# The output projection of a linear-attention stage in three bf16 passes, with its low half made first in GpSimd's step

## The chip, the cores and the metric

The kernel runs on one core of a Trainium2 chip. The metric is the device time of one execution in microseconds (us). A core has five engines with queues of their own: TensorE (PE; its weight loads are shown as PEld), VectorE (DVE), ScalarE (ACT), GpSimd (POOL) and SyncE (SP). Each works through its instructions strictly in order, and engines wait for one another by semaphores.

## The reference, cut to what matters

`x` is 128 sequences of 64 tokens with 256 channels, all f32. Two layers follow: L0 (attention and a feed-forward part, both with adaptive layer norm) and L1, a linear attention with a gated, modulated output:

```
xn = layer_norm(x, norm_g, norm_b)
q, k, v = xn @ Wq + bq, xn @ Wk + bk, xn @ Wv + bv      # 16 heads of 16 channels
q = softmax over the channels of a head;  k = softmax over the tokens
ctx = k^T v (per sequence and head);      y = q ctx
scale, shift = split(silu(emb) @ emb_W + emb_b)
h = layer_norm(y, sn_g, sn_b) * (1 + scale) + shift
h = silu(h) @ out_W + out_b                             # the projection that the change is about
x = x + gate_msa * h
```

## The kernel before, in words

Tokens lie on the 128 partitions, two sequences to a tile, so there are 64 tiles of 128 tokens by 256 channels. All of `x` stays on the core (`x_all`). Four stages follow each other: setup, an attention pass (to about 540 us), a feed-forward pass (to about 890 us), and the linear pass, `linear_pass`, for L1. A matmul whose operands are split into bf16 high and low halves runs as three passes, `SPLITS` = high by high, high by low, low by high.

In a pass, the order of work is a table written by hand for each engine. `pipeline(eng, [(lag, stage), ...])` walks over steps; in step s each listed stage, in the order of the list, is given tile s - lag. Since an engine keeps its order, the list is also the order in which its work queues up. Steps at both ends are written out, and those between run in a loop of four steps a turn.

In the linear pass, one step of each engine before the change is this (the number is the lag):

- TensorE: `k_v_first` 6 (L1545), `turn_kq` 5 (L1565, the transposes of the softmaxed k and q), `turn_x` 0 (L1594), `k_v_second` 6 (L1545), `project` 11 (L1515 and L1517), `qkv` 2 (L1573, L1576, then k in L1582, L1585), `q_kv` 7 (L1536), `turn_y` 8 (L1525).
- GpSimd: `softmax` 5 (L1403, L1405), `inverse_deviations` -1 (L1427, L1430), `silus` 10 (L1395, then L1397), `add` 12 (L1387).
- ScalarE: `x3_high` 1 (L1503), `v_high` 3 (L1497), `load_gate` 9 (issues two DMAs, L1443), `k_high` 5 (L1470), `q_copy` 5 (L1475), `k_exponentials` 3 (L1489), `modulate` 9 (L1458), `q_exponentials` 3 (L1479), `store` 13 (L1449), `tanhs` 9 (L1465).
- VectorE: `statistics`, `x3_low` 1 (L1709), `k_maxima`, `y_statistics`, `q_maxima`, `aggregate`, `q_lower`, `v_low`, `y_aggregate` 8 (L1620), `mask` 6 (L1633), `k_low`, `hat` -1 (L1702), `total` 4, `y_hats` 8, `residual` 11 (L1607).

How the stages hang together: `turn_kq` waits for `softmax` of the same step. `k_high` waits for `turn_kq`. `x3_high` writes a buffer with two slots, and so waits until `qkv` of the step before has done with k (`k_done`). `x3_low` waits for `x3_high`. `inverse_deviations` waits for `y_aggregate` (the second of the two values that it turns is y's), `hat` for `inverse_deviations`, and `mask` for `k_v_second` of its step. `silus` computes (tanh + 1) * z; its result, f32, is the stationary operand of `project` against the f32 weights `w_out3`. The projection's weights are loaded by SyncE at the start of the feed-forward pass, straight into their place. In that pass, stage `split_qvk3` (in its step for block 2) splits the weights of q, v and k in two, the high half on ScalarE and the low half on VectorE.

Of the kernel before, what the change touches and what calls it, by code (L numbers as in the profile page):

```python
# [23 lines left out]
ALU = mybir.AluOpType  # L24
ACT = mybir.ActivationFunctionType
# [86 lines left out]
class Shared:  # L112


    def __init__(self, nc, ctx):
        def sb(name, shape, dt):
            return ctx.enter_context(nc.sbuf_tensor(name, shape, dt))
# [18 lines left out]
        self.w_out3 = sb("w_out3", [P, NC_, C], F32)  # L136
# [782 lines left out]
def feed_forward_pass(nc, m, wq, wk, wv, bq, bk, bv, out_w):  # L919
# [5 lines left out]
    with ExitStack() as ctx:  # L925
# [8 lines left out]
        biases3_high, biases3_mid = m.w_qkv[:, HI, 0, :], m.w_qkv[:, HI, 1, :]  # L934
        b_norm3_wide = m.fc_full[:, 6 * C:6 * C + NC_ * P].rearrange("p (c n) -> p c n", c=NC_)
# [16 lines left out]
        qvk3_here = sem("qvk3_here")  # L952
        qvk3_hi_made = sem("qvk3_hi_made")
# [38 lines left out]
        @block.sync  # L992
        def _(sp):
            sp.dma_start(m.w_out3[:], out_w.rearrange(CHUNKED, p=P)).then_inc(m.linear_here, 16)
            for k, source in enumerate((wq, wv, wk)):
                sp.dma_start(qvk3_full[:, :, k * C:(k + 1) * C], source.rearrange(CHUNKED, p=P)).then_inc(qvk3_here, 16)
            for k, source in enumerate((bq, bv, bk)):
                sp.dma_start(biases3[:, k * C:(k + 1) * C], source[None, :].to_broadcast([P, C])).then_inc(qvk3_here, 16)
            sp.wait_ge(m.linear_here, 16)
# [44 lines left out]
        def _(act):  # L1044
# [9 lines left out]
            def split_qvk3(t):  # L1054

                if isinstance(t.n, int) and t.n == 2:
                    act.wait_ge(qvk3_here, 16 * 6)
                    act.wait_ge(norm3_widened, 2)
                    for c in range(NC_):
                        act.activation(m.w_qvk3[:, HI, c, 0:2 * C], qvk3_full[:, c, 0:2 * C], ACT.Identity,  # L1060
                                       scale=m.g_norm3[:, c:c + 1]).then_inc(qvk3_hi_made, 1)
                        act.activation(m.w_qvk3[:, HI, c, 2 * C:3 * C], qvk3_full[:, c, 2 * C:3 * C], ACT.Identity,
                                       scale=minus_g_norm3[:, c:c + 1]).then_inc(qvk3_hi_made, 1)
# [86 lines left out]
        def _(dve):  # L1150
# [82 lines left out]
            def split_qvk3(t):  # L1233

                if isinstance(t.n, int) and t.n == 2:
                    dve.wait_ge(qvk3_hi_made, 2 * NC_)
# [32 lines left out]
def linear_pass(nc, m, cond, out):  # L1269
# [5 lines left out]
    with ExitStack() as ctx:  # L1275
# [30 lines left out]
        silu = sb("silu", [P, NC_, P])  # L1306
        gate = sb("gate", [P, C], F32, 4)
# [46 lines left out]
        silu_made = sem("silu_made")  # L1354
        out_done = sem("out_done")
# [27 lines left out]
        def _(pool):  # L1383
# [6 lines left out]
            def silus(t):  # L1390
# [3 lines left out]
                reuse(pool, out_done, t, 2)  # L1394
                pool.tensor_tensor(silu[a][:], tanh[a][:], z_t[a][:], ALU.mult).then_inc(silu_product, 1)  # L1395
                pool.wait_ge(silu_product, t.n + 1)
                pool.tensor_tensor(silu[a][:], silu[a][:], z_t[a][:], ALU.add).then_inc(silu_made, 1)  # L1397

# [26 lines left out]
            def power(a, which, nth):  # L1425
# [7 lines left out]
            pipeline(pool, [(5, softmax), (-1, inverse_deviations), (Y_LAG, last_inverse_deviations),  # L1433
                            (10, silus), (12, add)])

        @block.scalar
        def _(act):
# [38 lines left out]

            def q_exponentials(t):
# [21 lines left out]
            def x3_high(t):  # L1499
# [5 lines left out]
            pipeline(act, [(1, x3_high), (3, v_high), (9, load_gate), (5, k_high), (5, q_copy),  # L1505
                           (3, k_exponentials), (9, modulate), (3, q_exponentials), (13, store),
# [3 lines left out]
        def _(pe):  # L1510
            def project(t):
                a = t.slot(2)
                pe.wait_ge(silu_made, t.n + 1)
                reuse(pe, branch_made, t, 1)
                pe.matmul(ps_out[:], m.ones[:], m.rows_out3, start=True, stop=False)  # L1515
                for c in range(NC_):
                    last = pe.matmul(ps_out[:], silu[a][:, c], m.w_out3[:, c], start=False, stop=(c == NC_ - 1))  # L1517
# [79 lines left out]
            pipeline(pe, [(6, k_v_first), (5, turn_kq), (0, turn_x), (6, k_v_second), (11, project), (2, qkv), (7, q_kv),  # L1597
# [3 lines left out]
        def _(dve):  # L1601
# [103 lines left out]
            def x3_low(t):  # L1705
# [8 lines left out]
                           (11, residual)])  # L1714
# [45 lines left out]
```

## Time and profile before

| | |
|---|---|
| median of 3 runs | 1313.19 us (1313.13 to 1314.98) |
| the profiled execution's own time | 1312.1 us |
| its span, first to last instruction | 1310.4 us |
| busy: PE, PEld | 1172.7 us (89%), 858.6 us (66%) |
| busy: DVE, ACT, POOL | 943.8 us (72%), 783.9 us (60%), 844.5 us (64%) |
| mean granted TensorE clock | 0.975 of full speed |

The busy figures are means over stages that differ much. Matmuls are pipelined and their ends are modelled, so what a matmul costs in a stream is read from the starts of neighbouring groups rather than from its own duration. On the other engines a record's duration can overlap the next start by some hundredths of a microsecond, so there too spacings between starts are the better measure. An idle time in brackets stands ahead of the instruction that ended it, with the one that released it.

### The profile page before, as it was taken

What the parts mean: (1) busy time and instruction counts of PE and PEld (TensorE: products, weight loads), DVE (VectorE), ACT (ScalarE), POOL (GpSimd) and SP (SyncE); (2) the same over time, 40 slices, a digit from 0 to 9 for tenths busy, and PEclk for the clock granted to TensorE, in tenths of its full rate; (3) what the DMA queues carried; (4) which work ended last, traced back from release to release, by engine and by line L of the source; (5) the groups of instructions that cost most, each with busy time, mean ns of one, the idle gap of its engine ahead of it and who ended that gap; (6) DMA issues with size and microseconds to landing.
All of it is one profiled execution on the core that took longest, in us unless ns stands there. A gap on an engine that the chain in (4) does not pass through costs nothing. (4 is left out here: it accounts for less than half of the span.)

```text
span 1310.4 us, 37657 instructions
## 1 busy us (share of the span) xinstructions
PE 1172.7 (89%) x12222; PEld 858.6 (66%) x12222; DVE 943.8 (72%) x2272; ACT 783.9 (60%) x2143; POOL 844.5 (64%) x1017
## 2 busy tenths in 40 slices
PE   3687889899899874999999999986999999999996
PEld 2466777777777763566666666663666666666664
DVE  6666788788788754646464656435899999999984
ACT  2666677677677762635454544523676676776764
POOL 4577677777777764546666667532466676676667
PEclk8899999999999997899999999997999999999999
DMA  7562323323323332000101010100011111111112
GB/s 243 142 147 50 60 57 55 61 55 56 65 51 59 60 56 72 17 28 22 33 16 32 16 32 16 33 17 1 17 39 37 40 52 37 39 52 39 45 48 73
DMA packets 138511, 67.85 MB, mean 52 GB/s; under 512 B 76368, under 2 KB 137168, under 8 KB 138448
## 3 DMA queue, kind: packets, MB, share of 16 engines
q1 hardware_dynamic: 109904, 40.92, 14.6%
q10 hardware_dynamic: 28544, 26.12, 6.6%
q8 instruction: 35, 0.57, 0.2%
q14 instruction: 28, 0.23, 0.1%
HBM read 41.31 MB, written 8.65 MB: 38 GB/s over the span
## 5 line engine op out<-in xcount | busy, mean ns | idle before, releaser
L1123 PE MATMUL f_ps_h<-f_x_split,w_fc 128*128 128x512 bf16 x768 | 173.2, 383 | 2.2 <-DVE f_biases L1249 1.2
L1096 PE MATMUL f_ps_y<-w_fc,f_h_split 128*128 128x256 bf16 x1536 | 172.7, 273 | 2.3 <-DVE f_branch L1215 2.3
L1096 PEld LDWEIGHTS f_ps_y<-w_fc,f_h_split 128*128 128x128 bf16 x1536 | 150.2, 98 | 23.6 <-issue 3.0
L634 POOL TENSOR_TENSOR e_split<-e_full,e_split 128x1024 bf16<-128x1024 f32 x64 | 136.5, 2134 | 33.5 <-ACT e_full L707 32.3
L1223 DVE TENSOR_TENSOR f_h_split<-f_h,f_h_split 128x512 bf16<-128x512 f32 x64 | 64.1, 1004 | 103.9 <-ACT f_h L1082 103.9
L1123 PEld LDWEIGHTS f_ps_h<-f_x_split,w_fc 128*128 128x128 bf16 x768 | 75.5, 99 | 88.9 <-issue 3.0
L1081 ACT ACTIVATE f_h_split<-f_ps_h,columns 128x512 bf16<-128x512 f32 x128 | 89.0, 695 | 66.3 <-POOL f_h_split L1038 36.3
L767 PE MATMUL ps_s<-qk_t,k_pairs 128*128 128x64 bf16 x3072 | 102.4, 195 | 12.7 <-DMA k_pairs<-qk_t 10.6
L767 PEld LDWEIGHTS ps_s<-qk_t,k_pairs 128*128 128x128 bf16 x3072 | 99.8, 99 | 15.5 <-DMA k_pairs<-qk_t 12.2
L614 POOL TENSOR_TENSOR x_split<-x_t,x_split 128x256 bf16<-128x256 f32 x64 | 44.5, 695 | 95.3 <-ACT x_split L655 95.3
L1427 POOL TENSOR_TENSOR l_rstd<-l_mean_var,eps_norm 128x2 f32<-128x2 f32 (+1 forms) x73 | 14.1, 193 | 140.2 <-DVE l_mean_var L1620 108.9
L1038 POOL TENSOR_TENSOR f_h_split<-f_h,f_h_split 128x512 bf16<-128x512 f32 x64 | 79.7, 1256 | 36.5 <-ACT f_h L1082 36.5
L786 PE MATMUL ps_qk<-w_qkv,x_split 128*128 128x512 bf16 x384 | 95.5, 386 | 0.4 <-POOL x_split L614 0.4
L1576 PE MATMUL l_ps_qv<-w_qvk,l_x_split 128*128 128x512 bf16 x384 | 95.8, 387 | 0.0
L1082 ACT ACTIVATE f_h<-f_ps_h,columns 128x512 f32<-128x512 f32 x128 | 89.5, 699 | 0.0
L1069 ACT ACTIVATE f_x_split<-f_x 128x1024 bf16<-128x1024 f32 x16 | 16.9, 1058 | 118.6 <-POOL f_x L1005 114.5
L1458 ACT ACTIVATE l_z_t<-l_ps_yt,shift,scale 128x64 f32<-128x64 f32 x256 | 84.4, 441 | 4.7 <-PE l_ps_yt L1525 3.7
L667 ACT ACTIVATE v_split<-ps_v 128x256 bf16<-128x256 f32 x64 | 24.7, 386 | 101.5 <-DMA v_pairs<-v_split 80.9
L702 ACT ACTIVATE e_split<-ps_s,minus_shift 128x1024 bf16<-128x1024 f32 x64 | 71.4, 1115 | 12.8 <-PE ps_s L767 12.5
L1489 ACT ACTIVATE l_kq<-l_ps_k,l_k_tops 128x64 f32<-128x64 f32 x256 | 77.0, 327 | 0.6 <-DVE l_k_tops L1655 0.5
L1470 ACT ACTIVATE l_k_t<-l_ps_kq 128x256 bf16<-128x256 f32 x64 | 24.5, 383 | 88.0 <-PE l_ps_kq L1565 87.9
L707 ACT ACTIVATE e_full<-ps_s,minus_shift 128x1024 f32<-128x1024 f32 x64 | 70.9, 1107 | 0.0
(182 smaller groups left out, 3285.3 us busy)
## 6 DMA issues: line engine op xcount, KB each, us to landing
v_pairs<-v_split SPq DMA_DIRECT2D x128, 66.0 KB, 2.1
k_pairs<-qk_t SPq DMA_DIRECT2D x256, 32.0 KB, 2.3
gain<-gammas SPq DMA_DIRECT2D x64, 128.0 KB, 3.0
f_gain<-gammas ACTq DMA_DIRECT2D x32, 256.0 KB, 4.2
l_gate<-in_cond ACTq DMA_DIRECT2D x128, 64.0 KB, 2.5
out<-x_all ACTq DMA_DIRECT2D x16, 512.0 KB, 3.0
x_all<-in_x SPq DMA_DIRECT2D x13, 512.0 KB, 5.4
fc_full<-in_L_cond_fc_w SPq DMA_DIRECT2D x2, 1024.0 KB, 7.6
```

Source lines behind the costliest of these rows:

```text
L634: pool.tensor_tensor(flat(e_split[a][:, LO]), flat(e_full[:]), flat(e_split[a][:, HI]), ALU.subtract).then_inc(e_lo_made, 1)
L702: act.activation(flat(e_split[a][:, HI]), flat(ps_s[:]), ACT.Exp, bias=m.minus_shift[:])
L767: last = pe.matmul(ps_s[:, s, G_ * c + g], k_pairs[:, t.slot(4), k, c, s, g].rearrange("p r k -> p (r k)"), qk_t[:, 0, t.slot(4), q, c, s ...
L786: last = pe.matmul(ps_qk[:, :], x1_split[a][:, xs, c, :], m.w_qkv[:, ws, c, 0:2 * C], start=(i == 0 and c == 0), stop=(i == 2 and c == NC_ ...
L1038: pool.tensor_tensor(h_split[a][:, LO, f], h[f % 4][:], h_split[a][:, HI, f], ALU.subtract).then_inc(h_lo_odd, 1)
L1081: act.activation(h_split[a][:, HI, f], ps_h[f % 4][:], ACT.Gelu, bias=m.b_fc1[:, f:f + 1])
L1082: act.activation(h[f % 4][:], ps_h[f % 4][:], ACT.Gelu, bias=m.b_fc1[:, f:f + 1]).then_inc(h_made, 1)
L1096: last = pe.matmul(ps_y[:, i], h_split[a][:, hs, f, i * P:(i + 1) * P], m.w_fc2[:, ws, f], start=(f == 0 and k == 0), stop=(f == F_CHUNKS ...
L1123: last = pe.matmul(ps_h[f % 4][:], m.w_fc1[:, ws, c, f * P:(f + 1) * P], x2_split[a][:, xs, c], start=(k == 0 and c == 0), stop=(k == 2 an ...
L1458: act.activation(z_t[a][:, c, s * L:(s + 1) * L], ps_yt[:, c, s * L:(s + 1) * L], ACT.Identity, bias=by_seq(m.shift3, c, t, s), scale=by_s ...
L1489: act.activation(kq[t.slot(4)][:, i * L:(i + 1) * L], ps_k[:, c, s * L:(s + 1) * L], ACT.Exp, bias=k_tops[a][:, c, s:s + 1], scale=-1.0, a ...
L1576: last = pe.matmul(ps_qv[:], x3_split[a][:, xs, c], m.w_qvk3[:, ws, c, 0:2 * C], start=False, stop=(i == 2 and c == NC_ - 1))
```

## The change

The f32 weights `w_out3` become a pair of bf16 halves. The f32 array is now loaded into `out3_full` in the feed-forward pass and split there, high half on ScalarE, low half on VectorE, ahead of the pieces of `split_qvk3`. In the linear pass the silu is split too: `silu_high` on ScalarE at lag 10, between `q_exponentials` and `tanhs`; `silu_low` on GpSimd at lag 11, as the first stage of its step. `project` then runs three bf16 passes over two chunks, six matmuls, in place of two f32 ones, and moves from lag 11 to 12; `residual` 11 to 12, `add` 12 to 13, `store` 13 to 14, `load_gate` 9 to 10.

```diff
-        self.w_out3 = sb("w_out3", [P, NC_, C], F32)
+        self.w_out3 = sb("w_out3", [P, 2, NC_, C], BF16)
...
-            sp.dma_start(m.w_out3[:], out_w.rearrange(CHUNKED, p=P)).then_inc(m.linear_here, 16)
+            sp.dma_start(out3_full[:], out_w.rearrange(CHUNKED, p=P)).then_inc(out3_here, 16)
...
-            sp.wait_ge(m.linear_here, 16)
+            sp.wait_ge(qvk3_here, 16 * 6)
...
                 if isinstance(t.n, int) and t.n == 2:
+                    act.wait_ge(out3_here, 16)
+                    act.activation(m.w_out3[:, HI], out3_full[:], ACT.Copy).then_inc(out3_hi_made, 1)
...
                 if isinstance(t.n, int) and t.n == 2:
+                    dve.wait_ge(out3_hi_made, 1)
+                    dve.tensor_tensor(m.w_out3[:, LO], out3_full[:], m.w_out3[:, HI], ALU.subtract)
...
                 pool.wait_ge(tanh_made, t.n + 1)
-                reuse(pool, out_done, t, 2)
+                reuse(pool, silu_lo_made, t, 2)
...
+            def silu_low(t):
+                a = t.slot(2)
+                pool.wait_ge(silu_hi_made, t.n + 1)
+                reuse(pool, out_done, t, 2)
+                pool.tensor_tensor(silu_split[a][:, LO], silu[a][:], silu_split[a][:, HI], ALU.subtract
+                                   ).then_inc(silu_lo_made, 1)
...
-            pipeline(pool, [(5, softmax), (-1, inverse_deviations), (Y_LAG, last_inverse_deviations),
-                            (10, silus), (12, add)])
+            pipeline(pool, [(11, silu_low), (5, softmax), (-1, inverse_deviations), (Y_LAG, last_inverse_deviations),
+                            (10, silus), (13, add)])
...
+            def silu_high(t):
+                a = t.slot(2)
+                act.wait_ge(silu_made, t.n + 1)
+                reuse(act, out_done, t, 2)
+                act.activation(silu_split[a][:, HI], silu[a][:], ACT.Copy).then_inc(silu_hi_made, 1)
...
-            pipeline(act, [(1, x3_high), (3, v_high), (9, load_gate), (5, k_high), (5, q_copy),
-                           (3, k_exponentials), (9, modulate), (3, q_exponentials), (13, store),
+            pipeline(act, [(1, x3_high), (3, v_high), (10, load_gate), (5, k_high), (5, q_copy),
+                           (3, k_exponentials), (9, modulate), (3, q_exponentials), (10, silu_high), (14, store),
                            (9, tanhs)])
...
-                pe.wait_ge(silu_made, t.n + 1)
+                pe.wait_ge(silu_lo_made, t.n + 1)
                 reuse(pe, branch_made, t, 1)
                 pe.matmul(ps_out[:], m.ones[:], m.rows_out3, start=True, stop=False)
-                for c in range(NC_):
-                    last = pe.matmul(ps_out[:], silu[a][:, c], m.w_out3[:, c], start=False, stop=(c == NC_ - 1))
+                for i, (zs, ws) in enumerate(SPLITS):
+                    for c in range(NC_):
+                        last = pe.matmul(ps_out[:], silu_split[a][:, zs, c], m.w_out3[:, ws, c],
+                                         start=False, stop=(i == 2 and c == NC_ - 1))
...
-            pipeline(pe, [(6, k_v_first), (5, turn_kq), (0, turn_x), (6, k_v_second), (11, project), (2, qkv), (7, q_kv),
+            pipeline(pe, [(6, k_v_first), (5, turn_kq), (0, turn_x), (6, k_v_second), (12, project), (2, qkv), (7, q_kv),
```

How this moves the instructions: first GpSimd, in the steps written out just ahead of the loop. Before, a step there (`silus`, `add`, then the next step's `softmax` and the two instructions for the inverse deviations) reads

```order
L1395 TENSOR_TENSOR l_silu<-l_tanh,l_z_t 128x256
L1397 TENSOR_TENSOR l_silu<-l_silu,l_z_t 128x256
L1387 TENSOR_TENSOR x_all<-x_all,l_branch 128x256
L1403 TENSOR_TENSOR l_kq<-l_kq,l_sums 128x256
L1405 TENSOR_TENSOR l_kq<-l_kq,l_sums 128x256
L1427 TENSOR_TENSOR l_rstd<-l_mean_var,eps_norm 128x2
```

and with the change (line numbers are the changed kernel's)

```order
L1405 TENSOR_TENSOR l_silu<-l_tanh,l_z_t 128x256
L1407 TENSOR_TENSOR l_silu<-l_silu,l_z_t 128x256
L1397 TENSOR_TENSOR x_all<-x_all,l_branch 128x256
L1413 TENSOR_TENSOR l_silu_split<-l_silu,l_silu_split 128x256
L1420 TENSOR_TENSOR l_kq<-l_kq,l_sums 128x256
L1422 TENSOR_TENSOR l_kq<-l_kq,l_sums 128x256
L1444 TENSOR_TENSOR l_rstd<-l_mean_var,eps_norm 128x2
```

One subtraction, L1413, now stands between the last instruction of a step (the sum into `x_all`) and the softmax of the next.

Second, ScalarE in the same place, the end of a step and the start of the next. Before:

```order
L1470 ACTIVATE l_k_t<-l_ps_kq 128x256
L1475 ACTIVATE l_q_t<-l_ps_kq 128x256
L1489 ACTIVATE l_kq,l_sums<-l_ps_k,l_k_tops 128x64 x4
L1458 ACTIVATE l_z_t<-l_ps_yt,shift,scale 128x64 x4
L1479 ACTIVATE l_kq<-l_kq 128x256
L1465 ACTIVATE l_tanh<-l_z_t 128x256
L1503 ACTIVATE l_x_split<-l_ps_xt 128x256
```

and with the change

```order
L1487 ACTIVATE l_k_t<-l_ps_kq 128x256
L1492 ACTIVATE l_q_t<-l_ps_kq 128x256
L1512 ACTIVATE l_kq,l_sums<-l_ps_k,l_k_tops 128x64 x4
L1475 ACTIVATE l_z_t<-l_ps_yt,shift,scale 128x64 x4
L1502 ACTIVATE l_kq<-l_kq 128x256
L1498 ACTIVATE l_silu_split<-l_silu 128x256
L1482 ACTIVATE l_tanh<-l_z_t 128x256
L1526 ACTIVATE l_x_split<-l_ps_xt 128x256
```

The copy that makes the high half, L1498, stands behind `q_exponentials` and ahead of the tanh. On TensorE nothing changes its place within a step: the pair L1515, L1517 x2 becomes L1538, L1541 x6.

## Rows read from the trace of the kernel before

**Rows 1.** Busy time by stretch: start:end us, span, then each engine, clock, DMA.

```profile
core 0: us, PE busy (x) PEld busy (x) DVE busy (x) ACT busy (x) POOL busy (x), PEclk, DMA share, GB/s
...
540.00:800.00 260.00, 257.90 (x1782) 175.93 (x1781) 147.38 (x236) 127.91 (x208) 162.40 (x107) 1.00 0.09 25
...
1000.00:1050.00 50.00, 49.67 (x441) 34.09 (x439) 47.23 (x131) 35.55 (x149) 34.42 (x59) 1.00 0.16 48
```

**Rows 2.** Timeline of one steady step: start us, us, engine, line, op [idle before].

```profile
1009.58 0.66 PE L1565 MATMUL l_ps_kq<-ident,l_kq 128*128 128x128 f32 x4
...
1010.27 0.38 ACT L1470 ACTIVATE l_k_t<-l_ps_kq 128x256 bf16<-128x256 f32 x1 [1.37 <-PE l_ps_kq L1565]
...
1010.82 0.28 PE L1515 MATMUL l_ps_out<-bias_rows,ones 128*128 128x256 bf16 x1
...
1010.93 0.69 DVE L1633 TENSOR_TENSOR l_kv<-l_ps_kv,same_head 128x512 f32<-128x512 f32 x1
...
1011.03 0.19 POOL L1427 TENSOR_TENSOR l_rstd<-l_mean_var,eps_norm 128x2 f32<-128x2 f32 x1 [1.60 <-DVE l_mean_var L1620]
...
1011.81 0.38 PE L1573 MATMUL l_ps_qv<-bias_rows,ones 128*128 128x512 bf16 x1
...
1011.97 0.73 POOL L1395 TENSOR_TENSOR l_silu<-l_tanh,l_z_t 128x256 f32<-128x256 f32 x1
...
1012.04 0.81 DVE L1702 TENSOR_SCALAR l_x_hat<-x_all,l_mean_var,l_rstd 128x256 f32 x1
...
1012.77 0.73 POOL L1397 TENSOR_TENSOR l_silu<-l_silu,l_z_t 128x256 f32<-128x256 f32 x1
...
1013.43 0.47 ACT L1465 ACTIVATE l_tanh<-l_z_t 128x256 f32<-128x256 f32 x1
...
1014.15 0.61 POOL L1403 TENSOR_TENSOR l_kq<-l_kq,l_sums 128x256 f32<-128x256 f32 x1
...
1014.36 0.38 ACT L1503 ACTIVATE l_x_split<-l_ps_xt 128x256 bf16<-128x256 f32 x1 [0.46 <-PE l_ps_k L1585]
...
1014.72 0.62 POOL L1405 TENSOR_TENSOR l_kq<-l_kq,l_sums 128x256 f32<-128x256 f32 x1
1014.78 0.42 DVE L1709 TENSOR_TENSOR l_x_split<-l_ps_xt,l_x_split 128x256 bf16<-128x256 f32 x1 [0.18 <-ACT l_x_split L1503]
...
1015.59 0.66 PE L1565 MATMUL l_ps_kq<-ident,l_kq 128*128 128x128 f32 x4
...
1017.24 0.19 POOL L1427 TENSOR_TENSOR l_rstd<-l_mean_var,eps_norm 128x2 f32<-128x2 f32 x1 [1.90 <-DVE l_mean_var L1620]
```

**Rows 3.** Timeline of the feed-forward pass: a stream of bf16 matmuls of 256 columns.

```profile
822.33 5.40 PE L1096 MATMUL f_ps_y<-w_fc,f_h_split 128*128 128x256 bf16 x48
```

**Rows 4.** Costliest groups, form by form: like operations; xcount, busy us, mean ns, idle before.

```profile
L655 ACT ACTIVATE x_split<-x_t 128x256 bf16<-128x256 f32 x64 | 26.2, 410 | 0.1
...
L1060 ACT ACTIVATE w_qvk<-fc_full,columns 128x512 bf16<-128x512 f32 x2 | 1.5, 750 | 0.0
...
L1223 DVE TENSOR_TENSOR f_h_split<-f_h,f_h_split 128x512 bf16<-128x512 f32 x64 | 64.1, 1004 | 103.9 <-ACT f_h L1082 103.9
...
L614 POOL TENSOR_TENSOR x_split<-x_t,x_split 128x256 bf16<-128x256 f32 x64 | 44.5, 695 | 95.3 <-ACT x_split L655 95.3
```

**Rows 5.** Timeline, ScalarE: the k copy of steps 11 and 66, 55 steps apart.

```profile
943.34 0.38 ACT L1470 ACTIVATE l_k_t<-l_ps_kq 128x256 bf16<-128x256 f32 x1 [1.96 <-PE l_ps_kq L1565]
...
1277.51 0.38 ACT L1470 ACTIVATE l_k_t<-l_ps_kq 128x256 bf16<-128x256 f32 x1 [1.90 <-PE l_ps_kq L1565]
```

**Rows 6.** Timeline, the last steps of the pass.

```profile
1301.66 0.72 POOL L1397 TENSOR_TENSOR l_silu<-l_silu,l_z_t 128x256 f32<-128x256 f32 x1
...
1303.83 0.72 POOL L1397 TENSOR_TENSOR l_silu<-l_silu,l_z_t 128x256 f32<-128x256 f32 x1
...
1304.60 0.28 PE L1515 MATMUL l_ps_out<-bias_rows,ones 128*128 128x256 bf16 x1 [1.02 <-POOL l_silu L1397]
...
1305.79 0.42 DVE L1607 TENSOR_TENSOR l_branch<-l_ps_out,l_gate 128x256 f32<-128x256 f32 x1 [1.74 <-PE l_ps_out L1517]
```

**Rows 7.** Timeline of an early step of the pass, where GpSimd is idle beside it.

```profile
928.23 0.41 DVE L1702 TENSOR_SCALAR l_x_hat<-x_all,l_mean_var,l_rstd 128x256 f32<-128x256 f32 x1 [0.27 <-POOL l_rstd L1430]
```

More of the change, by code:

```diff
@@ L934, in feed_forward_pass @@
         biases3_high, biases3_mid = m.w_qkv[:, HI, 0, :], m.w_qkv[:, HI, 1, :]
+        out3_full = sb("out3_full", [P, NC_, C], F32, 1)[0]
         b_norm3_wide = m.fc_full[:, 6 * C:6 * C + NC_ * P].rearrange("p (c n) -> p c n", c=NC_)
@@ L952, in feed_forward_pass @@
         qvk3_here = sem("qvk3_here")
+        out3_here = sem("out3_here")
+        out3_hi_made = sem("out3_hi_made")
         qvk3_hi_made = sem("qvk3_hi_made")
@@ L1306, in linear_pass @@
         silu = sb("silu", [P, NC_, P])
+        silu_split = sb("silu_split", [P, 2, NC_, P], BF16)
         gate = sb("gate", [P, C], F32, 4)
@@ L1354, in linear_pass @@
         silu_made = sem("silu_made")
+        silu_hi_made = sem("silu_hi_made")
+        silu_lo_made = sem("silu_lo_made")
         out_done = sem("out_done")
@@ L1713, in _ @@
                            (6, mask), (5, k_low), (-1, hat), (4, total), (Y_LAG, y_hats),
-                           (11, residual)])
+                           (12, residual)])
 _INS = ["x", "cond_1024", "L0_cond_mat_qkv_w", "L0_cond_q_bias", "L0_cond_v_bias", "L0_cond_scale_mul",
```

## The prediction

> **What bounds the kernel now.** I read the busy times by stretch first, since the page's means mix four stages. In the linear pass TensorE is busy 49.67 of 50 us and VectorE 47.23; ScalarE (35.55) and GpSimd (34.42) look as if they had room [rows 1]. The reader should not stop there: where GpSimd has its room decides this case. The timeline of one step, read next, shows it [rows 2]. GpSimd works without a break from L1427 (start 1011.03) through the silu, the sum and the two softmax products, whose last ends at 1014.72 + 0.62 = 1015.34. Then it idles 1.90 us, until VectorE has y's mean, and starts the next L1427 at 1017.24. All its slack lies *behind* the softmax. TensorE's transposes L1565, which wait for that softmax, start at 1015.59, a quarter of a microsecond after it. So an instruction put ahead of the softmax has 0.25 us of cover, and one put behind it would have 1.9 us.
>
> From one L1565 to the next it is 1015.59 - 1009.58 = 6.01 us; over the 55 steps from 11 to 66 the mean is (1277.51 - 943.34) / 55 = 6.08 [rows 2, 5]. I follow one further ring, because it passes through all engines and takes two steps: L1565 to `x3_high` (which ScalarE starts when TensorE has done with k: 0.46 us idle ahead of it) is 1014.36 - 1009.58 = 4.78; to `x3_low` 0.42; to the next L1427 1017.24 - 1014.78 = 2.46; L1427 to the softmax 1014.15 - 1011.03 = 3.12; the softmax itself 1.19 (1014.15 to 1015.34); GpSimd to TensorE 0.05 (in the last steps L1515 starts at 1304.60, and L1397, from 1303.83 for 0.72, ends at 1304.55 [rows 6]). The sum is 12.02, two steps, or 6.01 a step [rows 2]. So this ring stands level with TensorE's own stream: whatever is added to it shows, halved, in every step.
>
> **The change, part by part.**
>
> *TensorE's gain.* The projection takes 1011.81 - 1010.82 = 0.99 us of the stream, bias row included [rows 2]. A bf16 matmul of the same 256 columns costs 5.40 / 48 = 0.11 us in a stream [rows 3]; seven (bias and six) are 0.77. Gain 0.22 us a step, which shortens TensorE's stream to 5.79 and the 4.78 of the ring to 4.56.
>
> *GpSimd's subtraction.* The same form, 128x256 f32 into bf16, takes 0.695 us [rows 4]; records overlap the next by some 0.04 (1014.72 - 1014.15 = 0.57 for a product of 0.61), so 0.66. It stands ahead of the softmax, past the 0.25 us of cover. Of the ring above it makes 12.02 - 0.22 + 0.66 = 12.46, or **6.23 us a step**.
>
> *The new wait.* `silu_low` also waits for `silu_high`, and behind it in GpSimd's queue stand the softmax, and behind that L1565. This closes a ring of one step that was not there: L1565 to `k_high` 1010.27 - 1009.58 = 0.69; `k_high` to the place of `silu_high`, where L1465 starts now, 1013.43 - 1010.27 = 3.16; `silu_high` itself 0.41 (an f32 SBUF tile of that size into bf16 on ScalarE [rows 4]); to GpSimd about 0.08; the subtraction 0.66; the softmax 1.19; to TensorE 0.05. Sum **6.24 us a step** [rows 2, 4]. The 0.08 is an estimate between the 0.05 above and the 0.1 or so that L1427 lags behind VectorE. Bounds of this ring: 6.15 with 0.38 for `silu_high` (as L1503 takes from PSUM) and the subtraction hidden to 0.61, 6.32 with 0.47 (as L1465 takes).
>
> `silu_high`'s own input is in time: the silu is complete 1012.77 + 0.73 - 1011.03 = 2.47 us after L1427, and ScalarE comes to it 3.85 us after L1565, which is some 1.2 to 1.4 us ahead of L1427. ScalarE gives `silu_high` some 0.3 us, taken from the 0.46 that it idles ahead of `x3_high`; with k done 0.22 us earlier the two nearly meet, and I cost it at nothing. Were that cover gone, `x3_low` would be late and VectorE with it.
>
> *Both rings* give 6.23 and 6.24. The steady pass ran 0.07 above its ring before (6.08 against 6.01, loop turns and waits that alternate). TensorE and ScalarE now have slack over a loop turn, so I add only part of that, 0.05: 6.29. Over 55 steps: 55 x (6.29 - 6.08) = **+11.6 us**. The bounds for it, 6.15 and 6.45, are +4 and +20.
>
> *The drain.* In the last steps GpSimd alone sets the pace: silu products start 1303.83 - 1301.66 = 2.17 us apart, three instructions of 0.72 [rows 6]. Each such step gains 0.66; I count five, 3.3 us. The last tile's silu now goes through `silu_high` and `silu_low` before it is projected: 0.08 + 0.41 + 0.08 + 0.70 = 1.27, less the 0.22. Together **+4.3 us**, bounds 1 (the subtractions hidden) and 6 (seven steps).
>
> *The weights' split* in the feed-forward pass: one ScalarE copy, 0.75, and one VectorE subtraction, 1.0 [rows 4]. TensorE is busy 257.9 of 260 us there while ScalarE has 127.9 and VectorE 147.4 [rows 1], so their idle time hides both; 0, and 1.8 if not. SyncE's load goes elsewhere at the same time: 0. The lags of `residual`, `add`, `store` and `load_gate` move with `project`; their number and place in a step stay, so they cost nothing beyond the drain.
>
> *Sum*: +11.6 + 4.3 = +15.9 on the profiled 1312.1 us is 1328.0; on the median, 1.1 us higher, **1329.1 us**, 1.2% slower.
>
> **Rivals.**
>
> *TensorE stays the bound (faster).* If the softmax had more cover than I read, each step would drop by up to 0.22: 55 x 0.22 = 12 us gained, 4 lost in the drain, about 1305. For it: TensorE's 49.67 of 50. Against it: GpSimd has no idle time between L1427 and the softmax, and the ring's 6.01 leaves no room for 0.66. It decides from an uncovered delay under 0.2 us.
>
> *A draw.* The phases shift so that each step stays at 6.08, and the drain is half hidden: 1313 to 1315. The same would be seen if loading the longer straight code or the split hid all else. Nothing speaks for it but that GpSimd idles 1.9 us a step.
>
> *VectorE's hat is shut out (much slower).* L1702 takes 0.41 us beside an idle GpSimd [rows 7] and 0.81 beside the silu's first product, ending at 1012.85, 0.15 after that product's end [rows 2]: it gets through only in the gap between two GpSimd instructions. Its place hangs on `mask`, which follows `k_v_second` and so the later softmax. Now it arrives at 1012.04, product at 1011.97 to 1012.70. I expect it some 0.2 us later against the product; from 0.65 later it misses the gap and ends 0.80 (1012.77 - 1011.97) later. VectorE's spare before `x3_low` takes 0.2 of that, the rest is 0.6 a step in perhaps half of the steps: +16, about 1345. The Trainium skill, "SBUF — State Buffer", section "Who interferes with whom", has the rule: VectorE in a 2-port mode and GpSimd exclude each other for a whole instruction, and whoever comes second fully blocks. By that rule the trace agrees for the product; the added subtraction itself lies beside VectorE work that reads PSUM, so by the same rule it would block nothing.
>
> *Clock.* TensorE's granted clock is 1.00 in this stretch [rows 1], the upper level; its busy share should fall to some 5.79 / 6.29 = 0.92 and I expect the clock to stay. It is on my rings for only part, so a small drop costs a few us; this is in the range.
>
> **How the numbers follow.** A measurement tells 0.2%, 2.6 us, from no change. My forecast 0.85; faster 0.06; draw 0.04; hat shut out 0.05. Lower end: 4 + 1, with 1313.19 about 1318; I take 1316 for a shorter subtraction. Upper end: 20 + 6 + 2 gives 1341; I take 1343, part way to the hat's case. The drain alone is near 0.3%, so nearly all of my forecast is slower than 0.2%: slower 0.90, same 0.04, faster 0.06.
>
> **What would show it.** Right: L1565's successor starts within 0.1 us of the softmax's end in nearly each step, some 6.3 us apart; TensorE idle 0.3 to 0.6 us ahead of it, put down to GpSimd; GpSimd's idle ahead of the first rstd instruction down to about 1.3 us, and a short idle ahead of `silu_low` put down to ScalarE; the projection 0.77 us of stream. Wrong: steps of 6.0 us or less, TensorE still without waits; or the hat at over 1.2 us; or a feed-forward pass that is longer.

## The result and the profile after

The changed kernel takes 1334.35 us in the median of 4 runs (1331.79 to 1337.19), the one before 1313.16 us. The ratio is 1.0163, with a 95% interval of 1.0144 to 1.0182: it is slower by 1.6%. The profiled execution took 1331.79 us, with a span of 1330.1 us.

The page of the changed kernel: busy times, and the chain that ended last.

```profile
span 1330.1 us, 38024 instructions
...
PE 1157.0 (87%) x12197; PEld 854.4 (64%) x12350; DVE 941.7 (71%) x2273; ACT 801.9 (60%) x2208; POOL 888.3 (67%) x1081
...
POOL 9%; ACT 8%; issue 7%; PE 4%; DVE 4%; ACTq 0%; POOLq 0%; DVEq 0%
```

and the same chain in the kernel before:

```profile
PE 27%; DVE 2%; POOL 1%; issue 1%; ACT 0%; POOLq 0%; DVEq 0%; ACTq 0%
```

TensorE has 15.7 us less work than before (1172.7), GpSimd 43.8 us more (844.5), and the span is 19.7 us longer. The chain is led by GpSimd and ScalarE, no longer by TensorE.

Where the time went is read from two starts of the same instruction, the k copy on ScalarE, in step 11 and in step 66 (timeline of the changed kernel, as [rows 5]).

```profile
943.61 0.38 ACT L1487 ACTIVATE l_k_t<-l_ps_kq 128x256 bf16<-128x256 f32 x1 [1.80 <-PE l_ps_kq L1590]
...
1290.39 0.38 ACT L1487 ACTIVATE l_k_t<-l_ps_kq 128x256 bf16<-128x256 f32 x1 [2.06 <-PE l_ps_kq L1590]
```

Step 11 is reached 0.27 us later, which is nothing against what executions differ by there (see the note ahead of the experiments). The 55 steps take 346.78 us against 334.17: **6.305 us a step against 6.076, +12.6 us**. What follows step 66 takes 1330.1 - 1290.39 = 39.7 us against 32.9: **+6.8 us**.

The timeline of one steady step of the changed kernel, the instructions that answer to [rows 2]:

```profile
1012.38 0.66 PE L1590 MATMUL l_ps_kq<-ident,l_kq 128*128 128x128 f32 x4 [0.49 <-POOL l_kq L1422]
...
1013.07 0.38 ACT L1487 ACTIVATE l_k_t<-l_ps_kq 128x256 bf16<-128x256 f32 x1 [1.59 <-PE l_ps_kq L1590]
...
1013.62 0.28 PE L1538 MATMUL l_ps_out<-bias_rows,ones 128*128 128x256 bf16 x1
...
1014.61 1.46 PE L1601 MATMUL l_ps_qv<-w_qvk,l_x_split 128*128 128x512 bf16 x6
1014.66 0.76 DVE L1727 TENSOR_SCALAR l_x_hat<-x_all,l_mean_var,l_rstd 128x256 f32 x1
...
1015.35 0.72 POOL L1407 TENSOR_TENSOR l_silu<-l_silu,l_z_t 128x256 f32<-128x256 f32 x1
...
1016.04 0.73 POOL L1397 TENSOR_TENSOR x_all<-x_all,l_branch 128x256 f32 x1
1016.24 0.47 ACT L1498 ACTIVATE l_silu_split<-l_silu 128x256 bf16<-128x256 f32 x1
...
1016.78 0.67 POOL L1413 TENSOR_TENSOR l_silu_split<-l_silu,l_silu_split 128x256 bf16<-128x256 f32 x1
1016.95 0.38 ACT L1526 ACTIVATE l_x_split<-l_ps_xt 128x256 bf16<-128x256 f32 x1
...
1017.98 0.62 POOL L1422 TENSOR_TENSOR l_kq<-l_kq,l_sums 128x256 f32<-128x256 f32 x1
...
1018.66 0.66 PE L1590 MATMUL l_ps_kq<-ident,l_kq 128*128 128x128 f32 x4 [0.41 <-POOL l_kq L1422]
```

Follow it from the top. The k copy starts 0.69 after the transposes, `silu_high` (L1498) 3.17 after that and ends at 1016.71. `silu_low` (L1413) starts 0.07 later. The second softmax product ends at 1018.60, and the transposes of the next step start 0.06 later, 6.28 us after those of this one. TensorE has idled 0.41 us ahead of them. The silu is complete at 1016.07, in time for `silu_high`.

Both rings of the prediction end at `silu_low`, nearly together: behind the sum L1397 GpSimd is free again 0.69 us after its start (the spacing of these two instructions in e7, where `silu_low` has no such wait), at 1016.73, and `silu_high` lets it go at 1016.78. Over the 46 such pairs between 950 and 1250 us the spacing is 0.78 us on average, so the subtraction waits for ScalarE some 0.1 us a step.

The waits of the same stretch of the pass (950 to 1250 us; total us, times, longest) say it in sums:

```profile
ACT l_k_t L1487 <- PE l_ps_kq L1590: 84.2, 48, 1.9
POOL l_rstd L1444 <- DVE l_mean_var L1645: 60.7, 48, 1.5
PEld l_ps_kq L1590 <- POOL l_kq L1422: 28.4, 47, 0.7
PE l_ps_kq L1590 <- POOL l_kq L1422: 20.3, 47, 0.5
```

Before, no wait of TensorE for the softmax appears in that list; now it does in 47 of 48 steps. GpSimd's idle time ahead of the first rstd instruction is 60.7 / 48 = 1.3 us, as forecast. The wait of `silu_low` for `silu_high`, being so short, appears there only once, with 0.8 us.

### The profile page after: what moved, and what is told of

It reads as the page before. It is cut to its first block and busy times, and to the rows that moved or that the text cites. A ratio compares the mean times of both kernels' runs of the same rounds, so it can differ in the third digit from the quotient of the medians.

```text
span 1330.1 us, 38024 instructions
## 1 busy us (share of the span) xinstructions
PE 1157.0 (87%) x12197; PEld 854.4 (64%) x12350; DVE 941.7 (71%) x2273; ACT 801.9 (60%) x2208; POOL 888.3 (67%) x1081
## 5 line engine op out<-in xcount | busy, mean ns | idle before, releaser
L1128 PE MATMUL f_ps_h<-f_x_split,w_fc 128*128 128x512 bf16 x737 | 165.4, 381 | 5.0 <-DVE f_x_split L1194 1.9
L1041 POOL TENSOR_TENSOR f_h_split<-f_h,f_h_split 128x512 bf16<-128x512 f32 x64 | 79.8, 1256 | 36.2 <-ACT f_h L1087 36.2
L1601 PE MATMUL l_ps_qv<-w_qvk,l_x_split 128*128 128x512 bf16 x380 | 93.8, 382 | 4.9 <-DVE l_v_split L1705 1.6
L786 PE MATMUL ps_qk<-w_qkv,x_split 128*128 128x512 bf16 x323 | 83.3, 390 | 4.7 <-issue 0.9
```

What stands on the lines that cost most here:

```text
L786: last = pe.matmul(ps_qk[:, :], x1_split[a][:, xs, c, :], m.w_qkv[:, ws, c, 0:2 * C], start=(i == 0 and c == 0), stop=(i == 2 and c == NC_ ...
L1041: pool.tensor_tensor(h_split[a][:, LO, f], h[f % 4][:], h_split[a][:, HI, f], ALU.subtract).then_inc(h_lo_odd, 1)
L1128: last = pe.matmul(ps_h[f % 4][:], m.w_fc1[:, ws, c, f * P:(f + 1) * P], x2_split[a][:, xs, c], start=(k == 0 and c == 0), stop=(k == 2 an ...
L1601: last = pe.matmul(ps_qv[:], x3_split[a][:, xs, c], m.w_qvk3[:, ws, c, 0:2 * C], start=False, stop=(i == 2 and c == NC_ - 1))
```

## The experiments

A note for reading them: the start of step 11 (its k copy) lies between 939 and 948 us over the profiled executions, and differs by 8 us even between two whose code up to there is the same (939.42 in e8, 947.43 in e6). So I compare the steady steps (from step 11 to 66) and the rest after them within a profile, and times only as medians of several runs.

**e1: the subtraction behind the softmax.**

```diff
-            pipeline(pool, [(11, silu_low), (5, softmax), (-1, inverse_deviations), (Y_LAG, last_inverse_deviations),
+            pipeline(pool, [(5, softmax), (11, silu_low), (-1, inverse_deviations), (Y_LAG, last_inverse_deviations),
```

> Edit: the changed kernel with silu_low moved from ahead of the softmax to behind it in GpSimd's step; nothing else. Theory (the loss is the place of the subtraction, ahead of the softmax, while GpSimd's slack lies behind it): the softmax no longer waits for it nor for silu_high, the two-step ring is 12.02 - 0.22 = 11.80, so 5.9 us a step; TensorE's stream is 5.79 and VectorE's own work 5.7 to 5.9. Steps of 5.9 to 6.0 us from step 11 to 66, which is 0.3 less than the changed kernel's 6.30; the drain stays as the changed kernel's, 5 to 7 us over before. Time 1309 to 1315, within 0.3% of before. Rival (the new split costs by its mere amount of work on ScalarE and GpSimd, wherever it stands): steps stay at 6.2 to 6.3, time 1330.

1321.39 us, 1.0066 of before (1.0043 to 1.0089). The steps fall from 6.305 to (1283.77 - 945.35) / 55 = 6.153 us. TensorE's wait for the softmax is gone from the list. The direction is the theory's and its rival falls, but half of the expected gain is missing. The waits of e1 show two that the kernel before hardly had or did not have, one of TensorE for VectorE (0.4 us in one step before) and one of ScalarE:

```profile
PE l_ps_y L1561 <- DVE l_y_hat L1651: 12.6, 34, 0.5
ACT l_silu_split L1498 <- POOL l_silu L1407: 10.7, 33, 0.6
```

ScalarE now waits for the silu, with tanh and `x3_high` queued behind. That suggested a third ring, tested in e5.

**e2: the sum into x_all behind the softmax, the subtraction still first.** It shortens GpSimd's unbroken run and leaves the ring through ScalarE.

```diff
-            pipeline(pool, [(11, silu_low), (5, softmax), (-1, inverse_deviations), (Y_LAG, last_inverse_deviations),
-                            (10, silus), (13, add)])
+            pipeline(pool, [(11, silu_low), (5, softmax), (13, add), (-1, inverse_deviations), (Y_LAG, last_inverse_deviations),
+                            (10, silus)])
```

> Edit: the changed kernel with silu_low still first, but the sum into x_all (add) moved behind the softmax in GpSimd's step. This shortens the two-step ring by 0.69 (12.50 to 11.81, 5.9 a step) and leaves the one-step ring through ScalarE, silu_high, silu_low and the softmax as it is, 6.25 to 6.3. Theory (both rings are level): steps stay at 6.25 to 6.30, time 1328 to 1334, silu_low idles for ScalarE in nearly each step. Rival (only GpSimd's unbroken run from the inverse deviation to the softmax binds, the wait for silu_high is harmless): steps fall to 5.9 to 6.0 and the time to 1310 to 1315.

1334.04 us, 1.016 of before (1.013 to 1.019); (1290.67 - 944.00) / 55 = 6.303 us a step, the changed kernel's to 0.002. GpSimd got 0.69 us earlier to the subtraction and then waited:

```profile
POOL l_silu_split L1413 <- ACT l_silu_split L1498: 34.2, 47, 0.8
```

34.2 / 47 = 0.73 us each time: all that was gained, for nothing. So the one-step ring through `silu_high` alone holds the step at 6.3.

**e3: both behind the softmax.**

```diff
-            pipeline(pool, [(11, silu_low), (5, softmax), (-1, inverse_deviations), (Y_LAG, last_inverse_deviations),
-                            (10, silus), (13, add)])
+            pipeline(pool, [(5, softmax), (11, silu_low), (13, add), (-1, inverse_deviations), (Y_LAG, last_inverse_deviations),
+                            (10, silus)])
```

> Edit: the changed kernel with silu_low and add both behind the softmax in GpSimd's step. Theory: GpSimd and ScalarE are off every ring, TensorE (5.79) and VectorE (5.7 to 5.9) bound the step; 5.85 to 5.95 us, some 0.05 less than with silu_low alone behind it; time 1306 to 1313. Rival (VectorE's own pace, 5.9 to 6.0, is already the bound with silu_low alone behind the softmax): no difference from that run.

1322.14 us, 1.007 of before (1.0046 to 1.0094), steps of 6.144 us: like e1. The theory's 5.85 to 5.95 was wrong, and its time of 1306 to 1313 too. That there is no difference from e1 is what the rival says, but its reason, VectorE's own pace, falls with e5.

**e4: the kernel before with an idle subtraction.** The projection stays f32; there is no `silu_high`.

```diff
+            def extra(t):
+                pool.wait_ge(silu_made, t.n + 1)
+                reuse(pool, extra_made, t, 2)
+                pool.tensor_tensor(extra_out[t.slot(2)][:], silu[t.slot(2)][:],
+                                   m.ones[:, None, :].to_broadcast([P, NC_, P]), ALU.subtract).then_inc(extra_made, 1)
-            pipeline(pool, [(5, softmax), (-1, inverse_deviations), (Y_LAG, last_inverse_deviations),
+            pipeline(pool, [(11, extra), (5, softmax), (-1, inverse_deviations), (Y_LAG, last_inverse_deviations),
```

> Edit: the kernel before, with its f32 projection, and one more GpSimd subtraction of the same size (silu minus ones, into a tile that nobody reads) as first stage of its step; ScalarE and TensorE untouched. Theory: the two-step ring becomes 12.02 + 0.66 = 12.68, 6.34 a step against 6.08, so 55 x 0.26 = 14 us in the steady steps and 3 in the drain: about 1330, nearly all of the changed kernel's loss. Rival (the wait for silu_high on ScalarE is what costs): there is no such wait here, so steps stay at 6.1 and the time at 1313 to 1316.

1330.13 us, 1.0125 of before (1.0095 to 1.0156); (1295.51 - 948.24) / 55 = 6.314 us a step where 6.34 was worked out. (The profiled execution is a long one, 1335.88 us, but the excess lies mostly elsewhere: its step 11 starts 4.9 us later than that of the kernel before.) TensorE waits for the softmax here too (waits of e4):

```profile
PEld l_ps_kq L1573 <- POOL l_kq L1407: 17.8, 39, 0.7
```

So one subtraction on GpSimd at this place (0.63 us from its start to the next), with nothing else of the change, costs about what the steady steps lose, 0.24 us each; the two-step ring alone is enough as well.

**e5: high half behind x3_high too.** On top of e1:

```diff
-            pipeline(act, [(1, x3_high), (3, v_high), (10, load_gate), (5, k_high), (5, q_copy),
-                           (3, k_exponentials), (9, modulate), (3, q_exponentials), (10, silu_high), (14, store),
+            pipeline(act, [(1, x3_high), (3, v_high), (11, silu_high), (10, load_gate), (5, k_high), (5, q_copy),
+                           (3, k_exponentials), (9, modulate), (3, q_exponentials), (14, store),
```

> Edit: the kernel of e1 (silu_low behind the softmax), and on ScalarE silu_high moved from between q_exponentials and tanhs (lag 10) to behind v_high at the start of the next step (lag 11). In e1 the step is 6.15 us where 5.9 to 6.0 was expected; a third ring would explain it: inverse deviation to the finished silu 2.47, to silu_high 0.08, silu_high 0.33, tanh 0.31, x3_high to x3_low 0.42, x3_low to the next inverse deviation 2.46, in sum 6.07, plus loop turns. Theory: with silu_high behind x3_high this ring is gone, ScalarE starts x3_high when TensorE has done with k; steps of 5.95 to 6.05 us, 0.1 to 0.2 less than e1, time 1311 to 1316. Rival (VectorE's own work and loop turns are the bound in e1): steps stay at 6.10 to 6.15 and the time at 1321.

1312.38 us, 0.9997 of before (0.9986 to 1.0008); (1270.73 - 942.06) / 55 = 5.976 us a step, 0.18 under e1. ScalarE starts `x3_high` when TensorE is done with k again, as before the change. A step of e5:

```profile
1017.51 0.38 ACT L1526 ACTIVATE l_x_split<-l_ps_xt 128x256 bf16<-128x256 f32 x1 [0.19 <-PE l_ps_k L1610]
...
1018.05 0.42 ACT L1498 ACTIVATE l_silu_split<-l_silu 128x256 bf16<-128x256 f32 x1
...
1018.31 0.62 POOL L1422 TENSOR_TENSOR l_kq<-l_kq,l_sums 128x256 f32<-128x256 f32 x1
...
1018.89 0.67 POOL L1413 TENSOR_TENSOR l_silu_split<-l_silu,l_silu_split 128x256 bf16<-128x256 f32 x1
...
1020.81 0.19 POOL L1444 TENSOR_TENSOR l_rstd<-l_mean_var,eps_norm 128x2 f32<-128x2 f32 x1 [1.25 <-DVE l_mean_var L1645]
```

Both halves now lie in idle time: the high one on ScalarE ahead of the k copy, the low one on GpSimd between the softmax and the inverse deviation, where 1.25 us are still free. The third ring was what held e1 and e3. With it gone the projection's gain shows for the first time: 6.076 - 5.976 = 0.10 us a step, 5.5 us over 55. The drain takes 3.3 us of it back (36.2 us against 32.9). The profiled execution of e5 took 1308.68 us, 3.7 under its median, so the median, level with before, is not accounted for to the last 3 us.

**e6: no subtraction at all**, the high half in all three passes, so the low half is missing from the product. On top of e5:

```diff
-            pipeline(pool, [(5, softmax), (11, silu_low), (-1, inverse_deviations), (Y_LAG, last_inverse_deviations),
+            pipeline(pool, [(5, softmax), (-1, inverse_deviations), (Y_LAG, last_inverse_deviations),
...
-                        last = pe.matmul(ps_out[:], silu_split[a][:, zs, c], m.w_out3[:, ws, c],
+                        last = pe.matmul(ps_out[:], silu_split[a][:, HI, c], m.w_out3[:, ws, c],
```

> Edit: the kernel of e5 without silu_low: GpSimd's subtraction is left out and all three bf16 passes read the high half of the silu, so the low half of the silu is missing from the product; TensorE's work and ScalarE's copy are as in e5. It bounds what the shorter projection can give. Theory: GpSimd was off the rings in e5, so the steady steps are those of e5 within 0.03 us, and only the drain is shorter, by 3 to 4 us. Rival (GpSimd's extra work still costs in e5, through VectorE's hat or a later inverse deviation): steps are 0.05 us or more shorter than e5's.

1309.41 us, 0.9975 of before (0.996 to 0.9991), steps of 5.980 us, those of e5; what follows step 66 is 33.6 us against 36.2. So behind the softmax the subtraction is free in the steady steps and costs 2.6 us in the drain, a little under the 3 to 4 expected.

**e7: the low half a step later, still first.** Four buffers for the silu and its halves, so that `silu_low` never waits for `silu_high`.

```diff
-            pipeline(pool, [(11, silu_low), (5, softmax), (-1, inverse_deviations), (Y_LAG, last_inverse_deviations),
-                            (10, silus), (13, add)])
+            pipeline(pool, [(12, silu_low), (5, softmax), (-1, inverse_deviations), (Y_LAG, last_inverse_deviations),
+                            (10, silus), (14, add)])
...
-            pipeline(pe, [(6, k_v_first), (5, turn_kq), (0, turn_x), (6, k_v_second), (12, project), (2, qkv), (7, q_kv),
+            pipeline(pe, [(6, k_v_first), (5, turn_kq), (0, turn_x), (6, k_v_second), (13, project), (2, qkv), (7, q_kv),
```

> Edit: the changed kernel with silu_low still first in GpSimd's step but for lag 12, so that it never waits for silu_high; project, residual, add, store and load_gate one lag later each, four buffers for the silu and its halves. This opens the one-step ring through silu_high and leaves GpSimd's unbroken run (two-step ring of 12.5, 6.25 a step). Theory (each ring alone holds the step at 6.25 or more): steps 6.25 to 6.31, time 1331 to 1337 with one more step in the drain. Rival (only the wait for silu_high binds): steps fall to 6.1, time 1322 to 1325.

1331.89 us, 1.0136 of before (1.0112 to 1.016); (1290.69 - 946.83) / 55 = 6.252 us a step. Opening the one-step ring brings 0.05 us a step of the 0.23 lost; the two-step ring holds the rest.

**e8: e5 with add behind the softmax.**

```diff
-            pipeline(pool, [(5, softmax), (11, silu_low), (-1, inverse_deviations), (Y_LAG, last_inverse_deviations),
-                            (10, silus), (13, add)])
+            pipeline(pool, [(5, softmax), (11, silu_low), (13, add), (-1, inverse_deviations), (Y_LAG, last_inverse_deviations),
+                            (10, silus)])
```

> Edit: the kernel of e5 with add also behind the softmax on GpSimd (order softmax, silu_low, add). The two-step ring of e5 is 11.80, 5.90 a step, and falls to 11.1. Theory (VectorE and TensorE bound e5): steps as e5 within 0.03 us, time the same. Rival (the two-step ring still holds e5 up at loop turns): steps 0.03 to 0.1 us shorter.

1313.09 us, 1.0004 of before (0.9993 to 1.0016), steps of 5.972 us. GpSimd is no bound in the steady steps of e5. What follows step 66 is longer, though, 39.1 us against 36.2: with the sum behind the subtraction the drain's silu products start 3.36 us apart instead of 2.79.

**e9: e5 with the old lags.** There the low half is ready 0.7 us before its own step's projection, so the projection need not come a step later.

```diff
-            pipeline(pe, [(6, k_v_first), (5, turn_kq), (0, turn_x), (6, k_v_second), (12, project), (2, qkv), (7, q_kv),
+            pipeline(pe, [(6, k_v_first), (5, turn_kq), (0, turn_x), (6, k_v_second), (11, project), (2, qkv), (7, q_kv),
...
-                           (12, residual)])
+                           (11, residual)])
```

(likewise `add` 12, `store` 13, `load_gate` 9)

> Edit: the kernel of e5 (silu_low behind the softmax, silu_high behind v_high) with project and residual back at lag 11, add 12, store 13 and load_gate 9, as in the kernel before. In e5 silu_low ends 0.7 us before project of the same step starts, so the projection need not wait a step. Theory: steady steps as e5 (5.98), and one step fewer in the drain, 36.2 us in e5 against 32.9 before; some 1.5 to 3 us less: time 0.1 to 0.25% under the kernel before. Rival (the drain is set by GpSimd's total work alone, which this does not change, or project now waits for silu_low in the steady steps): the time of e5, level with before, or 1 to 3 us more.

1310.76 us, 0.998 of before (0.9966 to 0.9994): **the fastest kernel of the study that computes all of it**, 0.2% faster than the kernel before and 1.8% faster than the changed one (1310.76 / 1334.35). But not for the reason given. What follows step 66 is 36.1 us, as in e5, where 1.5 to 3 less were expected; the steady steps are a little shorter, (1272.96 - 945.44) / 55 = 5.955 us against 5.976, 1.2 us in all. Against e5 itself the gain is not clear of noise (the intervals of the two overlap); against before it is.

**e10: the last seven low halves on VectorE.** On top of e9:

```diff
+            def silu_low_late(t):
+                if isinstance(t.n, int) and t.n >= LATE:
+                    a = t.slot(2)
+                    dve.wait_ge(silu_hi_made, t.n + 1)
+                    reuse(dve, out_done, t, 2)
+                    dve.tensor_tensor(silu_split[a][:, LO], silu[a][:], silu_split[a][:, HI], ALU.subtract
+                                      ).then_inc(silu_lo_late, 1)
...
-                           (6, mask), (5, k_low), (-1, hat), (4, total), (Y_LAG, y_hats),
+                           (6, mask), (5, k_low), (11, silu_low_late), (-1, hat), (4, total), (Y_LAG, y_hats),
```

> Edit: the kernel of e9 with the low half of the silu of the last 7 tiles (57 to 63) made on VectorE, behind k_low in its step, in place of GpSimd. In the drain GpSimd is busy 9.5 of 10 us and VectorE 2 to 5. Theory (GpSimd's work sets the drain's pace): 7 subtractions of 0.66 leave it, the drain falls by 2 to 4 us against e9, to that of the kernel before or a little under: time 0.2 to 0.5% under before. Rival (the drain is the latency of the chain silu, high half, low half, projection, whoever makes the halves): within 1 us of e9.

1313.22 us, 1.0004 of before (0.999 to 1.0018), 2.5 us over e9, so both the theory and its rival missed. Of the profiled executions' difference, 2.1 us, 1.9 lie behind step 66 (38.1 us against 36.1). The work did move: in 1290 to 1300 GpSimd is busy 7.32 us in place of 9.61. But the granted clock of that stretch differs. Busy times by stretch of e10 (start:end, span, PE, PEld, DVE, ACT, POOL, clock, DMA):

```profile
1290.00:1300.00 10.00, 8.04 (x42) 4.82 (x41) 4.72 (x12) 4.96 (x15) 7.32 (x13) 0.51 0.09 30
```

and of e9:

```profile
1290.00:1300.00 10.00, 5.02 (x33) 2.94 (x33) 2.79 (x7) 6.26 (x18) 9.61 (x18) 0.85 0.26 89
```

The steady steps of the two are alike, so the loss lies in the drain, and beside it stands TensorE at its lower level. Whether the clock alone explains it, or also the latency of the chain that the rival names, these runs don't tell apart.

## Why the prediction was right

The forecast was 1329.1 us, slower; the measured 1334.35 lies 5 us above it and inside the range. The mechanism is the one that was forecast; its size was put a quarter too low (15.9 us forecast, 21.2 measured). By its steps:

- **What bounds the kernel, and where GpSimd's slack lies**: right. e4 shows it with nothing else changed, e1 and e5 by undoing it: with the same work on every engine, the place of two instructions in their queues moves the time from 1334 to 1312 us.
- **The gain on TensorE**, 0.22 us: right. From the projection's bias row L1538 to the six matmuls L1601 it is 1014.61 - 1013.62 = 0.99 us in the step shown; before, the same two starts were 1.20 apart (1010.82 for the bias row L1515, 1012.02 for the six matmuls L1576), so 0.21. But e5 turns only 0.10 of it into time. Its waits between 950 and 1250 us show what takes the rest: TensorE now waits for VectorE's y_hat, 4.9 us over 50 steps, 0.1 a step, and VectorE is busy 47.66 us of the 50 from 1000 on:

```profile
PE l_ps_y L1561 <- DVE l_y_hat L1651: 4.9, 23, 0.5
```

- **The two-step ring**, 6.23 a step: e7 leaves it alone in the changed kernel and measures 6.25; in the kernel before it was put at 6.34 and e4 measures 6.31.
- **The one-step ring**, 6.24: 6.28 in the step shown. The terms that are off nearly cancel: `silu_high` 0.47 for an estimate of 0.41, the subtraction 0.63 (1016.78 to 1017.41) for 0.66. That part is luck, of some hundredths. e2 leaves this ring alone and measures 6.30; e7, where it is open, 6.25. So in the changed kernel it is the longer of the two, by 0.05. The sign named for it, a short idle of GpSimd ahead of `silu_low`, came at 0.1 us a step, too short for the list of waits. Its upper bound, 6.32, is 6.30 by the terms given, and no row gives the 6.45 used for the range.
- **The allowance** of 0.05 for loop turns: it was 0.02 to 0.03 (6.305 on average, 6.28 in the step shown). 6.305 a step came out for 6.29, so +12.6 us for +11.6.
- **The cover of silu_high**: costed at nothing, with the words that its input is in time. In the changed kernel that holds, since the other rings are longer. But I called it slack, and it is a ring of its own, from the inverse deviation through the silu, `silu_high`, tanh, `x3_high` and `x3_low` back: 6.07 us and loop turns. e1 and e3 missed for its sake, and e5 showed it. The prediction's "in time" rests on TensorE's L1565 lying 1.2 to 1.4 us ahead of L1427. [rows 2] give 1.45 and 1.65, with which the silu would come 0.07 to 0.27 us after ScalarE. It is the changed kernel that has 1.23 (1012.38 to 1013.61), because its softmax is late; e1 makes the softmax early again, and there ScalarE waits. Nor was the idle time ahead of `x3_high` left over. It was all used up, and `x3_low` waits longer than before (2.1 us in 11 steps); the first line is of the kernel before, the second of the changed one, both 950 to 1250 us:

```profile
ACT l_x_split L1503 <- PE l_ps_k L1585: 20.5, 49, 0.5
DVE l_x_split L1734 <- ACT l_x_split L1526: 10.6, 35, 0.5
```

- **The weights' split** at nothing: 0.27 us up to step 11, far less than executions differ by, so a cost of a few us there could not be seen in one profile.
- **The drain**: the step that was mis-sized, +4.3 forecast and +6.8 measured. The subtraction's part was right: the silu products of the last steps start 1321.68 - 1318.89 = 2.79 us apart, for 2.17 + 0.66 = 2.83. Two things were left out: the one-step ring, which still holds as the drain begins, and TensorE's clock.

The ring first. The prediction let GpSimd alone set the pace of the drain. The changed kernel, steps 67 and 68:

```profile
1294.11 0.67 POOL L1413 TENSOR_TENSOR l_silu_split<-l_silu,l_silu_split 128x256 bf16<-128x256 f32 x1 [1.06 <-ACT l_silu_split L1498]
...
1295.98 0.66 PE L1590 MATMUL l_ps_kq<-ident,l_kq 128*128 128x128 f32 x4 [1.51 <-POOL l_kq L1422]
...
1296.67 0.38 ACT L1487 ACTIVATE l_k_t<-l_ps_kq 128x256 bf16<-128x256 f32 x1 [2.34 <-PE l_ps_kq L1590]
...
1302.86 0.38 ACT L1487 ACTIVATE l_k_t<-l_ps_kq 128x256 bf16<-128x256 f32 x1 [3.40 <-PE l_ps_kq L1590]
```

and of the kernel before:

```profile
1283.07 0.38 ACT L1470 ACTIVATE l_k_t<-l_ps_kq 128x256 bf16<-128x256 f32 x1 [1.93 <-PE l_ps_kq L1565]
...
1288.08 0.38 ACT L1470 ACTIVATE l_k_t<-l_ps_kq 128x256 bf16<-128x256 f32 x1 [2.73 <-PE l_ps_kq L1565]
```

From step 66 to 67 it takes 6.28 us, the ring's own length, against 5.56 before; now GpSimd's wait for `silu_high` is plain, 1.06 us. From step 67 to 68 it is 6.19 against 5.01, and there TensorE's clock has fallen. Together these two steps cost 1.9 us that the forecast did not have. What follows step 68 costs 4.9.

The end of the changed kernel's pass, busy times by stretch (columns as above):

```profile
1290.00:1296.00 6.00, 3.15 (x34) 2.06 (x32) 2.93 (x8) 3.94 (x17) 4.74 (x9) 1.00 0.09 17
1296.00:1302.00 6.00, 5.36 (x35) 3.49 (x36) 2.94 (x8) 2.56 (x8) 5.30 (x11) 0.59 0.08 26
1302.00:1308.00 6.00, 5.89 (x39) 3.76 (x37) 2.51 (x6) 3.55 (x12) 3.56 (x7) 0.56 0.10 23
...
1320.00:1327.00 7.00, 3.35 (x14) 1.77 (x14) 1.27 (x3) 0.78 (x3) 5.72 (x9) 0.50 0.28 94
```

and of the kernel before, its worst stretch of 6 us there and its last:

```profile
1283.00:1289.00 6.00, 5.80 (x42) 3.99 (x42) 3.49 (x9) 3.17 (x11) 4.48 (x8) 0.78 0.11 25
...
1301.00:1307.00 6.00, 2.72 (x12) 1.42 (x11) 1.27 (x3) 1.02 (x4) 5.46 (x8) 1.00 0.29 95
```

In the 6 us ahead of the fall TensorE was busy only 3.15 us; its longest waits there were 1.51 us for GpSimd's softmax and 1.34 us for VectorE's y_hat. Then it was granted half speed, the lower of its two levels, for some 10 us, and again at the very end. There it is late in a chain that nothing covers. Of the last tile, the last sum of the silu starts 3.80 us ahead of VectorE's product with the gate, before it was 1.96 [rows 6]:

```profile
1321.68 0.72 POOL L1407 TENSOR_TENSOR l_silu<-l_silu,l_z_t 128x256 f32<-128x256 f32 x1
...
1323.77 0.39 PE L1538 MATMUL l_ps_out<-bias_rows,ones 128*128 128x256 bf16 x1 [1.12 <-POOL l_silu_split L1413]
...
1325.48 0.42 DVE L1632 TENSOR_TENSOR l_branch<-l_ps_out,l_gate 128x256 f32<-128x256 f32 x1 [1.88 <-PE l_ps_out L1541]
```

From L1538 to L1632 it takes 1.71 us, where before it was 1.19 at the full clock and the new projection should need 0.22 less. So the last tile costs 1.84 us for a forecast of 1.27 - 0.22 = 1.05, and 0.74 of the 1.84 goes with the clock (the six matmuls L1541 take 1.49 us there, 0.82 in a steady step). The other 3.1 of the 4.9 us stand against the 3.3 that five steps were put at.

The steady steps kept a granted clock of 1.00, and TensorE was busy 0.92 of the time, both as expected:

```profile
1000.00:1050.00 50.00, 46.18 (x439) 32.25 (x445) 45.65 (x128) 36.35 (x152) 38.51 (x64) 1.00 0.14 42
```

Of the 5.25 us between forecast and median the profiled execution shows 3.8: 1.0 in the steady steps, 2.5 in the drain, 0.3 ahead of them. The rest is spread between runs: the changed kernel's profiled execution lies 2.6 us under its median, that of the kernel before 1.1 under its own.

**The rivals.** TensorE as the bound: no, it idles ahead of L1590 in 47 steps. A draw: no. VectorE shut out: in the step shown L1727 arrives 0.11 us after the first silu product started (1014.55) and takes 0.76 us; over 950 to 1250 us it takes 0.65 to 0.80. So it always got through in the first gap, this rival's point was never reached, and nothing here tests what would follow. One reading of that paragraph is off: VectorE's work beside the subtraction is not only work that reads PSUM, for the statistics L1714, which read `x_all` in SBUF, start at 1016.75, beside L1413.

## What to carry to other kernels

Where engines work through hand-ordered steps, an engine's idle share says little about where it can take work. Look for the instruction that ends each idle time: here the place just ahead of that wait was free (e5, e6), and the same instruction put ahead of the softmax delayed all that was queued behind it. Price such a change by following rings, from an instruction to the same one a step or two later, and write down every ring within some tenths of a microsecond of the longest; undoing the longest (e1) uncovered the next (e5). A ring that holds the steady steps can hold on into the drain, where everything else has become faster. And the split operand was cheap only with both halves in idle time: with them there, and the old lags, the same arithmetic went from 1.6% slower to 0.2% faster (e9).

## What the runs showed that was not expected

- The gain of the bf16 projection could not be had in full even with its halves made in idle time, or the low half left out: 0.22 us less on TensorE gave 0.10 to 0.12 us a step (e5, e6, e9).
- Taking GpSimd's work away in the drain (e10) made the kernel 2.5 us slower than e9, with TensorE at 0.51 of its clock in place of 0.85 over 10 us.
- The start of step 11 varies by 8 us between executions with the same code ahead of it (939.42 in e8, 947.43 in e6).
